# A banded attention and ternary feed-forward kernel: scores masked inside the second pass for all heads, a second layer ordered by high and low products, and small statistics moved to GpSimd

## The reference

```python
x = x + attn(layernorm(x), Wq, Wk, Wv, Wo)      # 16 heads of 16, causal, window of 64 tokens
x = x + ffn(layernorm(x), W1, b1, W2, b2)       # 256 -> 1024 -> 256, relu

allowed = (j <= i) & (j > i - 64)               # bias 0 where allowed, else -inf
scores = einsum('bhqd,bhkd->bhqk', q, k) / 4 + bias
out = einsum('bhqk,bhkd->bhqd', softmax(scores), v)

quantize(W) = clip(round(W / (mean(abs(W)) + 1e-5)), -1, 1)   # W1 and W2 become ternary
layernorm(x) = (x - mean) / sqrt(var + 1e-5)
```

## Time and profile before

| | us |
|---|---|
| median of 3 runs | 671.52 |
| the runs | 671.52, 671.65, 667.95 |
| the profiled execution, its own time | 669.85 |
| its span in the trace | 668.1 |

### The profile page before, as it was taken

The page is one execution under the profiler, slowest core; times in us unless marked ns, Lnnn a source line. Parts: engine busy times, 40 slices in busy tenths (PEclk is TensorE's granted clock), DMA queues, the critical chain, the costliest instruction groups (busy, mean ns, idle before and its releaser), DMA issues.

```text
span 668.1 us, 23907 instructions
## 1 busy us (share of the span) xinstructions
PE 645.6 (97%) x8049; PEld 556.4 (83%) x8049; DVE 610.4 (91%) x1389; ACT 565.0 (85%) x2483; POOL 562.2 (84%) x837
## 2 busy tenths in 40 slices
PE   8787899999999999999999999999999999998998
PEld 5475778889888888888888888888888898888887
DVE  7899899999989999898999999899999989898975
ACT  6788899898889989888998989899898989788723
POOL 8899999888889898888889888888988889798831
PEclk9979999999999999999999999999999999999999
DMA  9454444454453545444354544544454353344110
GB/s 307 111 126 87 122 79 98 100 129 107 94 120 81 126 96 128 108 95 117 82 126 98 137 98 96 120 87 121 95 138 98 66 133 70 100 90 100 36 49 32
DMA packets 187025, 70.19 MB, mean 105 GB/s; under 512 B 155284, under 2 KB 178454, under 8 KB 186904
## 3 DMA queue, kind: packets, MB, share of 16 engines
q1 hardware_dynamic: 155816, 41.27, 30.0%
q10 hardware_dynamic: 31088, 27.40, 13.6%
HBM read 20.35 MB, written 9.44 MB: 45 GB/s over the span
## 4 chain that ended last, share of the span: by engine, by line
PE 80%; DVE 7%; SPq 4%; issue 2%; DMA 2%; POOL 2%; ACT 1%; ACTq 1%; DVEq 0%; POOLq 0%
PE ps L1261 16%; PE ps L1248 14%; PE ps L1155 12%; PE ps L1133 11%; PE ps L1194 10%; PE ps L1221 6%; PE ps L1207 5%; SPq L353 2%; PE ps L1233 2%; PE ps L1125 2%; PE ps L1181 2%; SPq L325 2%; DVE negm L835 2%; PE ps L1256 1%; DVE pt L852 1%
## 5 line engine op out<-in xcount | busy, mean ns | idle before, releaser
L632 ACT ACTIVATE p<-ps,negm 128x96 f32<-128x96 f32 x1024 | 336.4, 358 | 13.4 <-DVE negm L835 12.7
L503 POOL TENSOR_TENSOR tl<-pt,th 128x384 f16<-128x384 f32 x256 | 235.2, 919 | 20.7
L632 ACT ACTIVATION_READ_ACCUMULATOR p<-ps,negm 128x1 f32 x1024 | 230.2, 225 | 0.0
L835 DVE TENSOR_REDUCE negm<-ps 128x4 f32<-128x384 f32 x256 | 137.7, 538 | 27.7 <-PE ps L1133 25.1
L501 POOL CAST th<-pt 128x384 f16<-128x384 f32 x256 | 128.9, 504 | 25.6 <-DVE pt L852 24.9
L852 DVE STREAM_TRANSPOSE pt<-p 128x384 f32<-128x384 f32 x256 | 143.5, 561 | 2.4 <-ACT p L632 2.2
L1133 PE MATMUL ps<-k,qbd 128*128 128x96 f16 x1536 | 124.0, 207 | 0.0
L1133 PEld LDWEIGHTS ps<-k,qbd 128*128 128x128 f16 x1536 | 112.1, 113 | 9.7
L1155 PE MATMUL ps<-th,vb 128*128 128x96 f16 (+1 forms) x1120 | 100.3, 204 | 0.0
L1155 PE MATMUL ps<-tl,vb 128*128 128x96 f16 (+1 forms) x1120 | 100.3, 205 | 0.0
L1248 PE MATMUL ps<-xTCh,w1T 128*128 128x256 f16 x512 | 97.6, 272 | 0.0
(11 more groups left out here) (151 smaller groups left out, 1406.4 us busy)
## 6 DMA issues: line engine op xcount, KB each, us to landing
k<-kst SPq DMA_DIRECT2D x32, 288.0 KB, 3.8
rwide<-parked ACTq DMA_DIRECT2D x32, 256.0 KB
qbd<-qs SPq DMA_DIRECT2D x252, 32.0 KB, 2.5
vb<-vd SPq DMA_DIRECT2D x248, 32.0 KB, 2.0
out<-x ACTq DMA_DIRECT2D x31, 256.0 KB, 2.1
x<-in_L_attn_hidden ACTq DMA_DIRECT2D x15, 512.0 KB, 4.8
kw<-kst SPq DMA_DIRECT2D x30, 192.0 KB, 4.0
k<-kst SPq DMA_DIRECT2D x32, 144.0 KB, 3.5
```

The source lines that it names most:

```text
L503: e.tensor_tensor(tl[g % 2][:, o], pt[n % 3][:, :], th[g % 2][:, o], ALU.subtract).then_inc(s_lo, 1)
L632: ins = e.activation(p[:, 96 * u:96 * u + 96], bank[:, 96 * u:96 * u + 96], ACT.Exp, bias=m[:, u:u + 1], accum_out=r[:, u:u + 1])
L835: e.tensor_reduce(negm[n % 4][:, :], sbank[n % 3][:, 0:384].rearrange("p (a b) -> p a b", b=96), AX.X, ALU.max, negate=True).then_inc(s_mx, 1)
```

## The change

Five things are done at once.

1. **Scores.** From chunk 1 on all four head groups mask in the second pass. `qm` and `kw` exist for both halves and all four groups; the 256-column mask matmul stays in chunk 0 alone, the 384-column one where it was.
2. **Placing.** `qm` is no longer filled from `qs` by four DMAs, but by one DMA per half that copies the 64 even partitions of `qbd` (8 KB each, 512 KB) once the high queries have landed there (`copy_q`); SP waits for them. Keys take four DMAs for each half.
3. **Second layer.** The first call runs bias and high products of both tiles, the second the low products of both. The very last half chunk stays by tiles.
4. **Statistics.** The two small operations move from DVE to GpSimd, as `tensor_scalar`, with a wait on `bn_aggr` ahead of them.
5. **Tables.** Values, the second `wo`, key half 1, the DMAs, the norms and the start-up masks change slots. GpSimd writes four `kw` and two `qm` patterns in place of two and one.

```diff
-V_LATE = 10
-A_T, A_K, A_Q, A_V = (1, 2), (5, 14), (6, 15), (10, 13)
-A_STATS, A_RSTD, A_NORM = (-24, -14), -12, (-7, -6)
+V_LATE = (8, 11)
+A_T, A_K, A_Q, A_V = (1, 2), (5, 13), (6, 15), (7, 9)
+A_STATS, A_RSTD, A_NORM = (-24, -14), -10, (-4, -5)
...
-Q_DMA, K_DMA, V_DMA, A_CARRY = (8, 20), (15, 22), 18, 2
-C_WO, C_STATS, C_RSTD = (8, 11), (10, 14), (12, 16)
-C_T, C_F, C_Y = (12, 17), (14, 20), (18, 25)
+F_V = (6, 9)
+Q_DMA, Q_COPY, K_DMA, V_DMA, A_CARRY = (9, 17), (13, 19), (7, 16), 13, 1
+C_WO, C_STATS, C_RSTD = (8, 10), (10, 14), (12, 16)
+C_T, C_F, C_Y = (12, 17), (14, 20), (18, 26)
...
-OUT_DMA, X_DMA = (24, 31), 36
+OUT_DMA, X_DMA = (26, 33), 35
...
-PV_LAG, O_ADD, O_SPLIT = 8, 9, 15
-
-R_INV, R_PARK, R_WIDEN, R_MUL = 9, 10, 11, 14
+PV_LAG, O_ADD, O_SPLIT = 8, 9, 14
+
+R_INV, R_PARK, R_WIDEN, R_MUL = 9, 10, 12, 14
...
-W_WO, K_MASK = (-6, -2), (9, 12)
+W_WO, K_MASK, Q_MASK = (-7, -2), (5, 8, 11, 15), (-1, 11)
...
@@ -291,51 +292,44 @@
             for g in (2 * t + i for i in groups):
                 if c >= 1:
                     e.wait_ge(s_sc, 16 * (c - 1) + 4 * g + 4)
-                if c == 1 and t == 0:
+                if c == 1:
                     e.wait_ge(s_kw, g + 1)
                 w, src = 64 + CH, kst[c % 2][t][:, :, :].tensor
                 row = 64 * (g % 2) * 2 * w
-                if t:
-                    e.dma_start(ks[g][:, :, :].rearrange("p m n -> p (m n)"),
-                                bass.AP(tensor=src, offset=row, ap=[[2 * w, 64], [0, 2], [1, 2 * w]])).then_inc(d_k[g], 16)
+                e.dma_start(ks[g][:, :], bass.AP(tensor=src, offset=row, ap=[[2 * w, 64], [0, 2], [1, w]])).then_inc(d_k[g], 16)
+                if c:
+                    e.dma_start(bass.AP(tensor=kw[g][:, :, :].tensor, offset=0, ap=[[2 * 1536, 64], [1, 1536]]),
+                                bass.AP(tensor=src, offset=row + w, ap=[[2 * w, 64], [32, 16], [1, 96]])).then_inc(d_k[g], 16)
                 else:
-                    e.dma_start(ks[g][:, 0, :], bass.AP(tensor=src, offset=row, ap=[[2 * w, 64], [0, 2], [1, w]])
+                    e.dma_start(first_kl[g], bass.AP(tensor=src, offset=row + w, ap=[[2 * w, 64], [0, 2], [1, w]])
                                 ).then_inc(d_k[g], 16)
-                    if c:
-                        e.dma_start(bass.AP(tensor=kw[g][:, :, :].tensor, offset=0, ap=[[2 * 1536, 64], [1, 1536]]),
-                                    bass.AP(tensor=src, offset=row + w, ap=[[2 * w, 64], [32, 16], [1, 96]])).then_inc(d_k[g], 16)
-                    else:
-                        e.dma_start(first_kl[g], bass.AP(tensor=src, offset=row + w, ap=[[2 * w, 64], [0, 2], [1, w]])
-                                    ).then_inc(d_k[g], 16)
-
-
...
-            for i in parts:
-                to, v = ((qbd[t], 0), (qm, 0), (qbd[t], 1))[i]
-                if to is qm and (t == 1 or c == 0):
-                    continue
-                if to is qm and c == 1:
-                    e.wait_ge(s_zm, 1)
+            for v in parts:
                 e.wait_ge((s_ahi, s_alo)[v], 8 * c + 4 + 4 * t)
                 for h in range(4):
-                    e.dma_start(bass.AP(tensor=to[:, :, :, :, :].tensor, offset=(32 * h + v) * 4096 + 128 * h,
+                    e.dma_start(bass.AP(tensor=qbd[t][:, :, :, :, :].tensor, offset=(32 * h + v) * 4096 + 128 * h,
                                         ap=[[2 * 4096, 16], [512, 8], [1, 128]]),
-                                qst[t][32 * h:32 * h + 32, v, :]).then_inc(d_q[t], 16)
...
-        def queries_placed(c, t):
-            return 16 * (8 * (c + 1) + (0 if t else 4 * c))
...
+        def copy_q(e, c, t):
+            e.wait_ge(d_q[t], 64 * (c + 1))
+            if c == 1:
+                e.wait_ge(s_zm, t + 1)
+            to, src = (z[t][:, :, :, :, :].tensor for z in (qm, qbd))
+            e.dma_start(bass.AP(tensor=to, offset=0, ap=[[2 * 4096, 64], [1, 4096]]),
+                        bass.AP(tensor=src, offset=0, ap=[[2 * 4096, 64], [1, 4096]])).then_inc(d_qm[t], 16)
...
+                    c = stage_a(n, Q_COPY[t])
+                    if c is not None and c >= 1:
+                        copy_q(e, c, t)
...
-            def mask_queries():
+            def mask_queries(t):
                 e.wait_ge(d_s, 16)
-                e.tensor_copy(qm[:, :, :, :, :].rearrange("p g a j b -> p (g a) (j b)").bitcast(f32),
-                              pr[0][:, 0:256].unsqueeze(1).to_broadcast([128, 8, 256])).then_inc(s_zm, 1)
+                e.tensor_copy(qm[t][:, :, :, :, :].rearrange("p g a j b -> p (g a) (j b)").bitcast(f32),
+                              smask.bitcast(f32).unsqueeze(1).to_broadcast([128, 8, 256])).then_inc(s_zm, 1)
...
             def rstd_a(c):
                 m = c % 2
+                e.wait_ge(s_agA, c + 1)
+                e.tensor_scalar(meanA[:, :], mvA[:, :, 0], -1.0, None, ALU.mult)
+                e.tensor_scalar(veA[:, :], mvA[:, :, 1], 1e-5, None, ALU.add).then_inc(s_mvA, 1)
...
             def rstd_c(h):
                 m = h % 2
+                e.wait_ge(s_agC, h + 1)
+                e.tensor_scalar(meanC[:, :], mvC[:, :, 0], -1.0, None, ALU.mult)
+                e.tensor_scalar(veC[:, :], mvC[:, :, 1], 1e-5, None, ALU.add).then_inc(s_mvC, 1)
...
                 ins.then_inc(s_agA, 1)
-                e.wait_ge(s_agA, c + 1)
-                e.tensor_reduce(meanA[:, :], mvA[:, :, 0:1], AX.X, ALU.max, negate=True)
-                e.tensor_reduce(veA[:, :], mvA[:, :, 1:3], AX.X, ALU.add).then_inc(s_mvA, 1)
...
             def c_stats(c, u):
                 h = 2 * c + u
                 e.wait_ge(s_cdv, USE[c, f"wo{u}"] + 1)
+                if h >= 1:
+                    e.wait_ge(s_agC, h)
...
-                e.wait_ge(d_q[g // 2], queries_placed(c, g // 2))
-                e.wait_ge(d_k[g], 16 * NKD[g // 2] * (c + 1))
+                e.wait_ge(d_q[g // 2], 64 * (c + 1))
+                e.wait_ge(d_ql[g // 2], 64 * (c + 1))
+                if c:
+                    e.wait_ge(d_qm[g // 2], 16 * c)
+                e.wait_ge(d_k[g], 32 * (c + 1))
                 if first:
                     e.matmul(bank[:, 0:384], identb[:, :], maskf[:, :], start=True, stop=False, skip_group_check=True)
-                elif g >= 2 or c == 0:
+                elif c == 0:
                     ends = bank[:, 0:384].rearrange("p (u j k) -> p u j k", j=3, k=32)[:, :, 0:3:2, :]
...
                     for m in range(2):
-                        to = qm if g < 2 and m and c else qbd[g // 2]
-                        keys = (ks[g][:, m, 32 * blk:32 * blk + 96] if g >= 2 or not m else kw[g][:, blk, :] if c
+                        to = qm[g // 2] if m and c else qbd[g // 2]
+                        keys = (ks[g][:, 32 * blk:32 * blk + 96] if not m else kw[g][:, blk, :] if c
                                 else first_kl[g][:, 32 * blk:32 * blk + 96])
...
-                                       start=(g < 2 and c > 0 and not first and m == 0 and u == 0),
+                                       start=(c > 0 and not first and m == 0 and u == 0),
...
-            def c_y(c, h, t):
+            def c_y(c, h, part):
                 last = (c, h) == (NCH - 1, 1)
-                bank = c_bank(c, "f12") if last and t else free("C", c, f"y{h}")
-                o = slice(t * 256, (t + 1) * 256)
-                e.matmul(bank[:, o], ones[:, 0:128], bp[:, F:], start=True, stop=False)
-                for hp, done, count in ((0, s_chi, SPLIT), (1, s_cdv, USE)):
-                    for f in range(8):
-                        if f % 2 == 0:
-                            e.wait_ge(done, count[c, f"f{h}{f // 2}"] + 1)
-                        ins = e.matmul(bank[:, o], hT[hp][:, f, t * 128:(t + 1) * 128], w2T[:, f, :],
-                                       start=False, stop=(f == 7 and hp == 1))
-                if last and t == 0:
+                for t in ((part,) if last else (0, 1)):
+                    bank = c_bank(c, "f12") if last and t else c_bank(c, f"y{h}") if part else free("C", c, f"y{h}")
+                    o = slice(t * 256, (t + 1) * 256)
+                    if last or part == 0:
+                        e.matmul(bank[:, o], ones[:, 0:128], bp[:, F:], start=(last or t == 0), stop=False, skip_group_check=True)
+                    for hp, done, count in ((0, s_chi, SPLIT), (1, s_cdv, USE)):
+                        if not last and hp != part:
+                            continue
+                        for f in range(8):
+                            if f % 2 == 0:
+                                e.wait_ge(done, count[c, f"f{h}{f // 2}"] + 1)
+                            ins = e.matmul(bank[:, o], hT[hp][:, f, t * 128:(t + 1) * 128], w2T[:, f, :], start=False,
+                                           stop=(f == 7 and hp == 1), skip_group_check=True)
```

## The result

The changed kernel takes 680.35 us (median of 5 runs, 680.24 to 681.75) against 671.52 us before. The ratio is 1.0151, with a 95% interval of 1.0123 to 1.0179: slower by 1.5%. The forecast was 659.5 us, 12 us faster than before; it came out 8.8 us slower.

What follows compares the result with a forecast made beforehand. The prediction took PE's stream to bound the kernel from 95 to 560 us; -11.7 (masks) - 3.3 (placing) + 1 (statistics) + 3 (start-up) = -11.0 us took the profiled 669.85 to 658.9, median 659.5 us, range 652 to 668.

Steps and rivals of the forecast that it cites:

- What bounds the kernel: From 95 to 560 us PE is busy 464.66 of 465.00 us, so a matmul taken out shortens the time if others follow.
- The mask matmuls: PE's score groups: 114 mask matmuls of 0.11 us go, 106 counted, -11.7 us; a chunk falls from 38.78 to 37.94 us.
- The placing: Key and query DMAs issued by SP: keys and copy arrive before PE needs them, so its 3.3 us of waits go.
- The second layer: Second-layer calls on PE: same 34 matmuls per half, high products no longer wait behind DVE's late low ones; 0 us.
- The statistics: Small operations moved from DVE to GpSimd: 1.5 us more a chunk, barely fits; +1 us in all, bounds 0 and 6.
- break-even, 0.31 us: Time per added GpSimd operation, six a chunk, at which the claim that GpSimd becomes the bound decides.
- The start-up: Before the first chunk is through: GpSimd writes three more patterns, 4.8 us, plus 0.6 for first norms; +3 us taken.
- GpSimd becomes the bound: Rival: at 0.574 us per added GpSimd operation a chunk takes 39.5 us, the whole kernel 682 us; chance 0.05.
- Half the gain is given back: Rival: bursts on DVE or GpSimd, at 95 and 98% of the chunk, open 6 us of PE gaps; 665 us, chance 0.20.
- Not one gap in 465 us so far: PE's middle stretch: the prediction's argument against half the gain being given back.
- The copy: Rival: the query copy lands late, beyond 8.3 us; at 9.6 us it costs 20 us, giving 679 us; chance 0.05.

## Why the prediction was wrong, point by point

**What bounds the kernel.** "In this stretch a matmul taken out shortens the run, provided the others can follow": right as a condition, and the condition was not met. PE without a gap says that PE is a bound, not how far behind it the next one stands. In the stretch from slot 12 DVE stood level with it, as the 0.06 us between `hTl` and the y call show in all twelve chunks of the kernel before.

**The mask matmuls, -11.7 us.** The count was right, and 0.11 us each too: the five outside DVE's stretch gave 0.49 us. But only those shorten the chunk; the three inside gave nothing in the new order and 0.08 us in the old. In all -7.4 us in the new order, -5.8 in the old.

**The placing, -3.3 us.** No score group waits for `qm` or for keys any more, and the copy lands in 4.3 us (4.8 estimated):

```profile
qm<-qbd SPq DMA_DIRECT2D x30, 512.0 KB, 4.3
```

The mechanism was right. "Values are asked for earlier, and their products on PE moved forward with them: free" is **the step that failed first**. I costed what a moved step issues and who waits for it, but not what it leaves behind: the stretch that it came from has 1.3 us less of PE's work and only 0.7 us less of DVE's, which ends it. The stretch gave back 0.75 us of the 1.3 that the rest of the chunk took on. With stage C's moves this costs 9 us (1.35%): in the profiled run 6.4 in the twelve chunks and 4.4 in the start-up, with 2.0 back in the tail. The values' and keys' places alone cost as much (1.5%).

**The second layer, 0.** Right by itself. That it "makes DVE's lateness harmless" is wrong: the y call waits for its bank, which a late `hTl` of DVE frees, before its first matmul.

**The statistics, +1 us.** The operations were mis-sized by little: 0.237 and 0.219 us against 0.2, 1.8 us a chunk against 1.5. By the prediction's own break-even, 0.31 us for each added operation, 0.30 with its gap is just under it. But the sum over the chunk was the wrong measure: GpSimd has its own packed stretch, 244.58 to 259.3 us, with two statistics steps, both norms and an O split, and that one ends in PE's wait. In the twelve chunks it costs 2.3 us only, because it takes the place of the wait for DVE (the stretch from slot 12 is 12.04 us in place of 11.84). The rest of the 8 us, where +1 stood (bounds 0 and 6), comes at the two ends, for which the prediction had only 0.6 us for the first norms: 3.3 us in the start-up, and the last two chunks, where PE waits 3.1 us for `xnC` (0.7 us with the statistics on DVE). On the kernel before the same edit costs 3 to 6 us, and in its profiled run all at the two ends.

**The start-up, +3 us (0 to 4.8).** It was +7.7, and not from the patterns that I priced, but from the places (+4.4) and the statistics (+3.3), both contained in the 9 and the 8 us above. "GpSimd is the full engine" there was half of the reading: from 28 to 49.6 us DVE is busy 21.10 of the 21.60 us, more than GpSimd's 20.40. Which of the two sets the start-up no run shows.

**The rivals.** "GpSimd becomes the bound", 0.05, 682 us, names an engine that PE does wait for, and was refused on a chunk's average. That its time is nearly right is luck: it comes from 0.574 us for an added operation, where 0.22 to 0.24 were measured, and it has neither the cost of the places nor the masks that give less. "Half the gain is given back" comes nearest to the mechanism, gaps on PE from DVE and GpSimd, though not from the bursts it names; it priced them at 6 us, where PE stands 9.8 us in the twelve chunks alone. "Not one gap in 465 us so far" spoke for nothing: it was the old order's balance, and busy time could not show the small gaps. The copy was in time.

## What to carry to other kernels

In a software pipeline with several engines above 85%, ask for every stretch between two hand-overs, not for every chunk, which engine needs how long. Work moved out of a stretch where another engine sets the pace frees there only what it takes off that engine, and costs its full length where it goes; work taken out counts only where its engine sets the pace. Do not read the distance between two bounds from busy shares or from one engine's work alone: compare when the last operation of each ends at the hand-over, and the distances between the starts of matmuls. Then leave the work out, with nothing else moved, before building its replacement: that one run would have shown 5.8 us for the masks, not 11.7.

## What the runs showed of the hardware

A GpSimd `tensor_scalar` of 128 x 255 took 572 ns with (multiply, add) and scalars from `rstdC` and `shiftC`, and 1257 ns with (subtract, multiply) and the mean read from `mvC`. No run separates the operation from the operand. The small ones (128 x 2) took 217 to 240 ns in all 64 cases of the changed kernel, so none had a DVE transpose of 0.57 us to wait out within its own time.
